# Experts packed four in three tiles, in a written-out block that also makes the routing weights

## What is computed

```python
router_logits = x2d @ gate_w                       # 1024x256 @ 256x64, f32
routing_weights = softmax(router_logits)           # then the 8 largest, divided by their sum
for the experts e taken by a token:                # gate, up: 256x96; down: 96x256, in bf16
    g, u = x @ gate_proj[e], x @ up_proj[e]
    y_e = (silu(g) * u) @ down_proj[e]
out = sum over the token's experts of weight * y_e # as f32, then rounded to bf16
```

## Time and profile before

| what | value |
|---|---|
| median of three runs | 2651.7 us |
| the profiled execution: its own time, its span | 2660.67 us, 2658.6 us |
| PE, DVE, ACT, POOL busy over the span | 79%, 69%, 51%, 22% |
| router's first instruction to the next stage's first | 615.48 to 1111.49 us |
| DVE busy in a stretch of 50 us of the experts (705 to 755) | 50.00 us |
| TensorE's granted clock there | 0.60 of full speed |

### The profile page before, as it was taken

One profiled execution on the slowest core, in us unless ns is written; L12 is line 12 of the kernel. 1 busy time (PEld: TensorE's weight loads), 2 busy tenths in 40 slices (PEclk: granted clock), 3 DMA queues, 4 the chain that ended last, 5 costly groups with the idle time before them and its releaser, 6 DMA issues. The chain is left out here.

```text
span 2658.6 us, 35498 instructions
## 1 busy us (share of the span) xinstructions
PE 2099.5 (79%) x11529; PEld 1344.7 (51%) x11529; DVE 1832.5 (69%) x3840; ACT 1346.9 (51%) x2550; POOL 583.0 (22%) x689
## 2 busy tenths in 40 slices
PE   5999999975675566487586689567999999966978
PEld 3676676753332233255365335345667676742545
DVE  5877788765999899874588686548334353558835
ACT  4666666545887788534433336532434333341651
POOL 2332233312554454210253100111101010101000
PEclk8999999987666766578678779768999999985989
DMA  5000000001110210040320210023000000014000
GB/s 194 1 3 3 2 3 1 1 11 58 42 42 3 76 40 27 25 140 5 70 59 7 69 46 3 17 75 154 2 2 0 1 0 2 1 60 98 27 34 16
DMA packets 62766, 94.49 MB, mean 36 GB/s; under 512 B 9787, under 2 KB 56459, under 8 KB 60023
## 3 DMA queue, kind: packets, MB, share of 16 engines
q1 hardware_dynamic: 59340, 87.81, 10.6%
q0 software_dynamic: 1728, 4.22, 0.7%
q10 hardware_dynamic: 1536, 0.49, 0.1%
HBM read 80.53 MB, written 10.49 MB: 34 GB/s over the span
## 5 line engine op out<-in xcount | busy, mean ns | idle before, releaser
L1250 DVE SCALAR_TENSOR_TENSOR moe_acc<-moee_eo,moee_wt,moe_acc 128x256 f32<-128x256 bf16 x512 | 229.6, 514 | 0.3
L761 DVE SCALAR_TENSOR_TENSOR l_acc<-l_px,l0w_chan,l_acc 128x253 f32<-128x253 f32 (+2 forms) x288 | 137.5, 477 | 100.0 <-POOL l_acc L729 99.4
L1163 POOL TENSOR_TENSOR moee_hb<-moee_gb,moee_ub 96x1024 bf16<-96x1024 bf16 x64 | 146.9, 2296 | 228.3 <-DVE moee_gb L1257 228.3
L1176 PE MATMUL moee_pu<-moe_xb,moee_wb 128*96 128x512 bf16 x256 | 101.1, 537 | 100.6 <-DVE moee_ub L1232 100.6
L1212 ACT CAST moee_eo<-moee_po 128x512 bf16<-128x512 f32 x224 | 115.3, 594 | 80.6 <-PE moee_po L1187 80.6
L1187 PE MATMUL moee_po<-moee_db,moee_hb 96*128 96x256 bf16 x512 | 110.5, 389 | 45.0 <-DVE moee_eo L1241 27.5
L1176 PE MATMUL moee_pg<-moe_xb,moee_wb 128*96 128x512 bf16 x256 | 100.7, 536 | 34.0 <-POOL moee_db L1148 24.0
L3012 DVE SCALAR_TENSOR_TENSOR l3b_sz<-l3b_sig,l3b_pz 128x256 f32<-128x256 f32 x48 | 20.2, 421 | 142.3 <-ACT l3b_sig L2990 142.3
L350 PE MATMUL ln_pt<-ident,xn 128*128 128x128 f32 x176 | 40.6, 424 | 98.3 <-DVE xn L281 98.3
L1176 PEld LDWEIGHTS moee_pu<-moe_xb,moee_wb 128*96 128x96 bf16 x256 | 35.1, 161 | 163.9 <-DVE moee_ub L1232 141.6
L1662 ACT ACTIVATE l3xa_ex<-l3xa_pS 128x512 f32<-128x512 f32 x128 | 74.1, 605 | 85.9 <-PE l3xa_pS L1575 81.5
(11 more groups left out here) (623 smaller groups left out, 5894.8 us busy)
## 6 DMA issues: line engine op xcount, KB each, us to landing
moee_wf<-in_moe_up SPq DMA_DIRECT2D x64, 192.0 KB, 2.4
l3w_w_in<-in_l_w_in SPq DMA_DIRECT2D x1, 8224.0 KB, 26.0
m1b_bc<-bc_rows SPq DMA_DIRECT2D x16, 512.0 KB, 6.2
l0w_w_in<-in_l_w_in SPq DMA_DIRECT2D x1, 6448.0 KB
moee_df<-in_moe_down SPq DMA_DIRECT2D x64, 96.0 KB, 2.1
l_qs<-parts_q SPq DMA_DIRECT2D x36, 128.0 KB
l0w_w_out<-in_l_w_out SPq DMA_DIRECT2D x1, 3072.0 KB
parts_q<-l_pieces SPq DMA_DIRECT2D x16, 192.0 KB, 2.5
```

The lines of the kernel that those rows point to most:

```text
L761: nc.vector.scalar_tensor_tensor(out=a, in0=px[:, 0:S - (L0_CONV - 1 - c)], scalar=w, in1=a, op0=ALU.mult, op1=ALU.add).then_inc(tap_done, 1)
L1163: nc.gpsimd.tensor_tensor(hb[:, e % 3, :], gb[:, e % 4, :], ub[:, e % 4, :], ALU.mult).then_inc(h_done, 1)
L1176: last = nc.tensor.matmul(ps[0:MOE_F, half, :], wb[:, e % R, k, n * MOE_F:(n + 1) * MOE_F], xb[:, k, half * 512:(half + 1) * 512], start=( ...
L1250: last = nc.vector.scalar_tensor_tensor(out=acc[:, t, :], in0=eo[:, i % 2, t, :], scalar=wt[:, i, t:t + 1], in1=acc[:, t, :], op0=ALU.mult ...
```

## The change

**Packing.** Four experts of 96 hidden values lie in three tiles of 128: tiles 3n, 3n + 1 and 3n + 2 hold in partitions 0 to 95 experts 4n, 4n + 1 and 4n + 2, and in partitions 96 to 127 a third each of expert 4n + 3. So gate, up and everything on the hidden values runs over 48 tiles of 128 partitions and not 64 of 96. The outputs stay 64: the fourth expert's product is a sum of three with 32 rows each. `lay_out` reorders the weights on the host.

**Written out.** One block goes over the 48 tiles and 3 steps more; there are no turns. The output is handed over in quarters (`o_done` counts four per expert).

**Moved.** The min(1 + ex, 2^63) goes from VectorE to GpSimd, gb * ub from GpSimd to VectorE. The router's products, the softmax and the weights are made in the same block: VectorE does its part of it in three pieces, one ahead of each of its first three steps. The gate is loaded in the normalization. The end (rounding, adding to `res`) is inside the block too, tile by tile, with the rounding on ScalarE.

```diff
+        normalize(nc, g, [(gate[:, :, :], I["moe_gate"])])
+        with Stage(nc, "moee") as st:
+            R, H, U, LAG = MOE_RING, 9, MOE_N, 3
...
+            def pieces(e):
+                n, r = 3 * (e // 4), e % 4
+                return [(n + r, slice(0, MOE_F))] if r < 3 else [(n + i, slice(MOE_F, P)) for i in range(3)]
...
+                @block.gpsimd
+                def _(pool):
...
+                    for i in range(AHEAD):
+                        cast_weights(i)
+                    nc.gpsimd.memset(acc[:, :, :], 0.0).then_inc(zeroed, 1)
+                    for i in range(U):
+                        pool.wait_ge(exp_done, i + 1)
+                        nc.gpsimd.tensor_scalar(ex[:, i % 4, :], ex[:, i % 4, :], 1.0, MOE_BIG, ALU.add,
+                                                ALU.min).then_inc(one_plus, 1)
+                        if i + AHEAD < U:
+                            cast_weights(i + AHEAD)
...
+                        if i >= LAG:
+                            pe.wait_ge(h_done, i - LAG + 1)
+                            for e in experts(i - LAG):
+                                for q in range(4):
+                                    if e >= 1:
+                                        wait_evicted(pe, e - 1, q)
...
+                                    for t in range(2 * q, 2 * q + 2):
+                                        parts = pieces(e)
+                                        for n, (j, rows) in enumerate(parts):
+                                            last = nc.tensor.matmul(
+                                                po[:, t, :], hb[rows, j % H, t * P:(t + 1) * P], db[rows, j % H, :],
+                                                start=(n == 0), stop=(n == len(parts) - 1))
+                                    last.then_inc(o_done, 1)
...
+                    for i in range(U + LAG):
+                        if i < 3:
+                            routing(i)
...
+                        if 1 <= i <= U:
+                            j = i - 1
+                            dve.wait_ge(inv_done, j + 1)
+                            nc.vector.tensor_tensor(gb[:, j % 4, :], gb[:, j % 4, :], ex[:, j % 4, :],
+                                                    ALU.mult).then_inc(gated, 1)
+                            dve.wait_ge(gated, j + 1)
...
+                            nc.vector.tensor_tensor(hb[:, j % H, :], gb[:, j % 4, :], ub[:, j % 4, :],
+                                                    ALU.mult).then_inc(h_done, 1)
```

```diff
-    link(nc.vector.tensor_tensor(r, r, parts[1], ALU.subtract))
-    return nc.vector.tensor_copy(parts[2], r)
...
+                        if rotary:
+                            act.wait_ge(rotated, u + 1)
+                            if u >= 2:
+                                act.wait_ge(sent[u % 2], 32 * (u // 2))
+                            nc.scalar.copy(parts[0:width, u % 2, 0, :], qf[0:width, u % 2, :]).then_inc(first_done, 1)
...
+                    link(nc.vector.tensor_tensor(r, now, part[0], ALU.subtract))
+                    link(nc.vector.tensor_copy(part[1], r))
+                    nc.vector.tensor_tensor(part[2], r, part[1], ALU.subtract).then_inc(split_done, 1)
...
+                for u in range(len(units) + rotary):
+                    if rotary and u < len(units):
+                        rotate(u)
+                    if u >= rotary:
+                        split(u - rotary)
```

More of the change, by code:

```diff
@@ L40 @@
 SEM_CARRIED = 230
+SEM_MOE = 240
 class Stage:
@@ L1033, in mixture @@
         xb = wst.sbuf("xb", [P, KT, TOK], BF16)
[L1034 to L1096, removed]
@@ L1098, in mixture, with before, experts @@
-        with nc.Fori(0, MOE_E // MOE_UNROLL) as turn, Stage(nc, "moee") as st:
-            R, U = MOE_RING, MOE_UNROLL
-            LAG = 3
+        wf = wst.sbuf("wf", [P, MOE_RING, KT, 2, P])
+        df = wst.sbuf("df", [P, MOE_RING, D])
+        gate = wst.sbuf("gate", [P, KT, MOE_E])
+        loads = [nc.alloc_semaphore(f"moe_loaded{r}", num=SEM_MOE + r) for r in range(MOE_RING)]
+        normalize(nc, g, [(gate[:, :, :], I["moe_gate"])])
+        with Stage(nc, "moee") as st:
+            R, H, U, LAG = MOE_RING, 9, MOE_N, 3
+            LAST = MOE_E - 1
+            def before(i):
+                return 4 * (i // 3) + i % 3
+            def experts(i):
+                return range(before(i), before(i + 1))
+            def pieces(e):
+                n, r = 3 * (e // 4), e % 4
+                return [(n + r, slice(0, MOE_F))] if r < 3 else [(n + i, slice(MOE_F, P)) for i in range(3)]
@@ L1166, in _ @@
                 @block.tensor
                 def _(pe):
-                    for e in range(U + LAG):
-                        if e < U:
-                            pe.wait_ge(cast, e + 1)
+                    for t in range(NT):
+                        for k in range(KT):
+                            last = nc.tensor.matmul(pl[:, t, :], xT[:, k, t // ST, (t % ST) * P:(t % ST + 1) * P],
+                                                    gate[:, k, :], start=(k == 0), stop=(k == KT - 1))
+                    last.then_inc(logits, 1)
@@ L1260, in mixture @@
[L1260 to L1269 removed]
+                    link = in_order(dve, v_chain)
@@ L1274 @@
+                    for t in range(NT):
+                        dve.wait_ge(rounded, t + 1)
+                        nc.vector.tensor_tensor(res[:, t, :], res[:, t, :], accb[:, t, :], ALU.add)
 TOK = B * S
@@ L1405, in _, with table, by_s @@
                     dve.wait_ge(tables_in, 16 * len(tables_of))
-                for u, ((w, ws, bias, tables, src, out), half) in enumerate(units):
+                def table(a, width, half):
+                    if a.shape[1] == S:
+                        return a[0:width, None, :].broadcast_to([width, HALF // S, S])
+                    return a[0:width, half * HALF:(half + 1) * HALF].rearrange("p (b s) -> p b s", s=S)
+                def by_s(a):
+                    return a.rearrange("p (b s) -> p b s", s=S)
@@ new lines, in rotate, with split @@
+                    dve.wait_ge(taken, u + 1)
+                    nc.vector.tensor_tensor(now, now, t1[0:width, :], ALU.add).then_inc(rotated, 1)
+                def split(u):
+                    (w, ws, bias, tables, src, out), half = units[u]
+                    width = w.shape[2]
+                    now = qf[0:width, u % 2, :]
+                    r, part = rest[0:width, :], [parts[0:width, u % 2, n, :] for n in range(3)]
+                    if rotary:
+                        dve.wait_ge(first_done, u + 1)
@@ L1426, in _ @@
                     else:
                         dve.wait_ge(taken, u + 1)
+                    if u >= 1:
+                        dve.wait_ge(split_done, u)
                     if u >= 2:
                         dve.wait_ge(sent[u % 2], 32 * (u // 2))
-                    split3(nc, link, now, rest[0:width, :],
-                           [parts[0:width, u % 2, n, :] for n in range(3)]).then_inc(split_done, 1)
+                    if not rotary:
+                        nc.vector.tensor_copy(part[0], now).then_inc(first_done, 1)
+                        dve.wait_ge(first_done, u + 1)
```

319 lines of the change are left out of this document (166 added, 153 removed).

## The result

After takes 2557.03 us (median of four runs, 2547.14 to 2566.79), before 2651.61: a ratio of 0.9645, with a 95% interval of 0.9607 to 0.9683. That is 95 us faster, where 34 were forecast, and the time lies just under 2558, the lower end of the range. The profiled execution took 2566.79 us (span 2564.9).

A forecast was written before the change was run, and what follows sets the result against it. VectorE was taken to bound the mixture: 26.5 + 337 + 102 + 4.5 = 470 us against 496, 26 less; with 8 less in the projections, 34 less together, giving 2618 us, range 2558 to 2655.

The forecast's parts named there:

- its own work in the stretch: VectorE's work in the mixture from its first accumulate on, without what GpSimd blocks: 337 us.
- the fill: Mixture's start, from the router's first product to the first accumulate: 26.5 us, 2.6 of it softmax.
- The projections' sum: Attention projections outside the mixture: plain 3, third layer 3, cross 2 us less, 8 us together.
- 44 tiles x 2.63 x 0.88 = 102 us: Mixture: VectorE time blocked by GpSimd's min(1 + ex) and weight casts, 2.63 us a tile, share 0.88.
- loses GpSimd's duration less 0.23: Mixture: a VectorE accumulate stands still while GpSimd works, losing that instruction's duration less 0.23 us.
- Each us of the price is worth 38.7: Mixture: each us of GpSimd's min(1 + ex) duration changes the forecast time by 38.7 us.
- The price of min(1 + ex), 2.36: GpSimd's min(1 + ex) at 1024 elements: 2.62 us extrapolated from f32 rows, a tenth off for bf16.
- The high bound: GpSimd's min(1 + ex): a second pass for its second arithmetic step makes it 4.4 us.
- The first: Rival: GpSimd does min(1 + ex) at the casts' rate, 1.05 us; 51 less, 2567 us; chance 0.23.
- The second: Rival: GpSimd's op makes a pass per arithmetic step, 4.4 us, blocking accumulates; 2697 us, slower from 3.2; chance 0.13.
- The third: Rival: TensorE binds in every third step of the mixture, VectorE waiting 1.5 to 2 us; 2646 us; chance 0.12.
- The fourth: Rival: blocking spares one-input ops or falls on ub and eo; TensorE's 366 us binds; 2545 us; chance 0.05.

The follow-up runs named there:

- before_proj: before with only the new projections (project_heads) of after; 2645.4 us, ratio 0.9970 to before.
- op_copy: after with GpSimd's min(1 + ex) replaced by a plain copy of ex in place; 2563.2 us, ratio 0.9665 to before.
- op_half: after with GpSimd's min(1 + ex) on only the first 512 of the 1024 elements; 2529.9 us, ratio 0.9545 to before.
- lag_only: after with the longer distance of aligned between the pipeline's steps, but without its added wait on GpSimd; 2554.5 us, ratio 0.9634 to before.
- aligned3: aligned with GpSimd casting the weights three tiles ahead in place of two; 2561.9 us, ratio 0.9642 to before.
- aligned3_evict: aligned3 with ScalarE copying all four output quarters of every expert; 2549.8 us, ratio 0.9607 to before.
- oldroles_evict: after with min(1 + ex) back on VectorE, the product on GpSimd, and ScalarE copying all output quarters; 2548.6 us, ratio 0.9602 to before.
- aligned: after with a longer pipeline distance and GpSimd's min(1 + ex) waiting for the previous step's hb, to start beside ub; 2580.3 us, ratio 0.9726 to before.
- op_one_step: after with GpSimd's op only adding 1, without min; 2561.2 us, ratio 0.9657 to before.
- evict_act: after with ScalarE copying all four output quarters of every expert; 2526.3 us, ratio 0.9534 to before.

## Why the prediction was wrong

**Right**: the bound (VectorE busy throughout), its own work in the stretch (forecast 337 us, measured 376.3 - 42.3 - 2.2 = 332), the fill (26.5, measured 26.0), the end (4.5, measured 3.9). Rows of before carried these terms, but for the 2.6 of softmax in the fill, a judgement that came out. The projections' sum is right (8, by before_proj 8), by luck in its parts: 3, 3 and 2 were forecast, 1.7, 2.6 and 5.0 measured.

**Wrong**: the term "44 tiles x 2.63 x 0.88 = 102 us" of what GpSimd blocks. It measured 42, and these 60 us are nearly the whole miss of the mixture: 470 forecast, 406 measured. Of the 102, 82 stood for the op and 19 for the casts; 34 and 8 were measured. Two steps of the term failed.

1. The rule "loses GpSimd's duration less 0.23". It was read from a two-input product, for which reading and duration are nearly the same: 2048 elements read, 1.88 us lost, 2.12 long. For an op with one input and arithmetic they part: 0.78 lost in 3.7 us. op_copy has the loss with 1.04 us of length, op_half half the loss: VectorE loses 0.76 ns for each element that the op reads (0.92 for the product's), once. "Each us of the price is worth 38.7" made the forecast depend on the wrong quantity; the price drops out.
2. The price of min(1 + ex), 2.36, was 3.62 at the least. The extrapolated 2.62 for one step was near (2.76). A tenth off for bf16 was not, and the second step adds 0.85 us. The high bound was right that a second step costs time, but the 4.4 us that it gave were too many.

With the right price and the wrong rule the forecast would have been 2618 + 1.26 x 38.7 = 2667: the two errors stood against each other.

**The rivals.** The first (2567, the op at 1.05 us) came nearest, for a reason that did not hold: op_copy has that very duration and after's time. The second's condition held (3.8 us over 3.2) and its consequence did not. The third (TensorE binds) is refuted: VectorE is idle for 2 us, and TensorE busy 268 of 377 us where 366 were reckoned at the lower clock; the granted one was 0.69 on the mean. The fourth (2545) is refuted too: GpSimd's op has one input and costs VectorE 0.78 even so, and nothing fell on ub.

The Trainium skill, GPSIMD Engine Reference, section "Performance versus the Vector engine", puts a body of up to two operations at 1.03 cycles an element of 1.2 GHz. By that alone 1024 elements are an estimate of 0.88 us; the prediction said 1.1, which needs a start of some 0.2 on top, as the casts' rows have it (0.394 less 256 x 0.86 ns is 0.17). So read, the trace agrees for the copy (1.04 us); for add and min it does not (3.62).

What the prediction never asked was the size of the parts by themselves: packing 48 us, loop 24, router 14. Its sum held them, in the 337 and in the fill. But by the sum the loss, 91 us in before, would grow to 102; it fell to 59 with the roles, to 54 with the loop and to 42 with the packing.

**Open.** Several kernels end at a stretch of 370 to 377 us with quite different losses and idle times (after, lag_only, aligned3, aligned3_evict, oldroles_evict). For aligned3 the waits name ScalarE's quarters; whether one common chain stands behind all was not tried. Nor did a run show why the op reads its input in one piece: that it does is read from VectorE's lengths, not seen on GpSimd.

## What to carry to other kernels

Before an operation is moved to GpSimd, ask what it reads and what VectorE does when it starts. Its length matters for what waits behind it on GpSimd (aligned), not for what VectorE loses. Put it beside a VectorE instruction that reads PSUM, if the rhythm allows it without a new wait. Take the price of an instruction from a place where the other engine is idle: a duration from the middle of the stage can be three quarters loss (1.62 against 0.41). Work out each part of a change by itself before summing.

## What the runs showed of the hardware

- GpSimd's in-place op on 128 x 1024 bf16, at the shortest: copy 1.04 us (op_copy), add 2.76 (op_one_step), add and min 3.62 (after); on 512 elements, add and min 1.91 (op_half).
- VectorE's loss beside it: 0.35 us for 512 elements read, 0.78 for 1024, 1.88 for two times 1024, 0.35 and 0.14 for casts of 512 and 256. It falls on accumulates, gb and hb, which read two tiles from SBUF, and also on VectorE's min(1 + ex), which reads one (1.62 in place of 0.41 in before). ub, which reads PSUM, takes 1.20 to 1.23 us beside any of them. The Trainium skill, SBUF — State Buffer, section "SBUF: two separate sides", says that whichever of the two engines starts first holds the pair of ports that they share for the whole instruction. For the two-input product that comes near (1.88 us lost, 2.12 long); for the op of 3.7 us, which costs 0.78, the runs say otherwise.
- An edit on one engine moves the others' phase: evict_act gained 19 us that way, op_one_step lost 6.
